# Three-term float32r products for Wo, W4 and the last layer in a one-core GNN kernel, with graph operations, one-hot turns and warm-up matmuls moved

## Chip, cores and metric

One core of a Trainium2 chip (trn2) runs the whole program. The metric is the device time of one execution in microseconds (us). Differences of 0.2% are the finest that are spoken of.

## What is computed

Four graph layers in sequence on 128 nodes with 512 features and 4096 edges, each followed by a layer norm over `x + layer(x)`. All values are float32. Cut to what the change touches:

```python
# layer 0: attention over the graph (8 heads of 64), then
attn_out = attn_out @ Wo + bo
h1 = layer_norm(x + attn_out, g1, be1)
ff = relu(h1 @ W1 + b1) @ W2 + b2
# layer 1: edge network: h = mish(edge_feat @ W1 + b1); messages = mish(h @ W2 + b2)
agg = segment_sum(messages, dst)
u = mish(concat([x, agg]) @ W3 + b3)
out = u @ W4 + b4                      # then layer_norm(x + out)
# layer 2: two GCN convolutions, 512 -> 128 -> 512, with the normalised adjacency
# layer 3:
h_self = einsum("nd,od->no", x, W_self)
h_neigh = einsum("nd,od->no", neigh_mean, W_neigh)
h = layer_norm(h_self + h_neigh + bias) * gamma + beta
```

## The kernel before

The program is written by hand, one instruction list for each engine (`block.sync`, `block.gpsimd`, `block.scalar`, `block.tensor`, `block.vector`), and semaphores join them. There is no scheduler: each engine does its list in the order in which it stands in the code, and a wait holds everything behind it on that engine. Node rows lie on the 128 partitions. A matrix of 512 by 512 lies as four chunks of 128 rows.

**Kinds of product.** `columns_by(banks, lhs, rhs, h, cs, ...)` (L460 to L465) multiplies transposed activations by the half `h` (256 columns) of a weight matrix, over the chunks `cs`; a whole product of 512 by 512 is eight such matmuls, four for each half of the output. With float32 operands each matmul is two instructions in the trace. In the edge network the operands have already been split: a value v becomes `hi`, which is v rounded to float32r, and `lo = v - hi`, also written as float32r, and a product is the three terms hi·hi, hi·lo and lo·hi (L674 and L675, 512 columns a matmul, one instruction each). ScalarE writes the hi parts, VectorE subtracts for the lo parts.

**Start.** Five bf16 matmuls on the identity run on TensorE before x has arrived (`keep_warm(5, bank[2])`, L526, waiting for `ident_ready`); then come x transposed (L444), x added to the output banks (L458), Q and K (L537), the scores, V (L561), the counting of edges (L549), and the attention output (L573, L577), whose signal is `ao_done`.

**Around Wo.** VectorE copies the attention output in two halves (`aoT`, L927). TensorE turns one group of one-hots of the targets in the meantime (`turn_onehots(Dbf, range(1))`, L582), adds the bias rows (L584) and multiplies by Wo in float32 (L589), then turns the other seven groups (L594). Each group goes into one of four banks, ScalarE copies it to `DT` (L313), and group g (from 4 on) waits for the copy of group g - 4. VectorE, behind the two copies, does `features_low(0)` (L906), `Wclo` (L930), eight small operations on the graph matrices (L932 to L939), and only then the statistics of the first layer norm (L823), for which `wo_done` is awaited. GpSimd takes the inverse roots, the graph's first and then the norms' (L278 to L280).

**Edge network.** Eight groups of 512 edges, from 69 to 205 us. TensorE runs nearly without a pause in it.

**Tail.** u @ W4 in float32 (L748), a sum of G1 (L755), then W_self and W_neigh are turned by TensorE in eight steps (`turn`, L696), each copied by ScalarE (`turned_out`, L414), with the transposes of y between; the GCN layer (L767 to L783); then five warm-up matmuls (L787), the transposes of x (L452), the neighbour mean (L790), and the last layer in float32: `xT` by `WsT` (L795) and `nmT` by `WnT` (L798), whose inputs VectorE copies (L811, L1094). The rest is VectorE's norm and the store.

Buffers lie over each other in one region of 95 units of 512 columns; the maps are `first`, `other`, `last`.

```python
            for h in range(2):
                pe.wait_ge(S["ao_ready"], h + 1)
                for b in range(2):
                    done = columns_by(O_BANKS, aoT, Wo, b, (2 * h, 2 * h + 1), None, KC - 1)
```

Of the kernel before, what the change touches and what calls it, by code (L numbers as in the profile page):

```python
# [4 lines left out]
F32 = mybir.dt.float32  # L5
# [35 lines left out]
def gnn_kernel(nc, a, out):  # L41

    ctx = ExitStack()
    with ctx:
# [32 lines left out]
        ones2 = sb("ones2", [2, N], F32R)  # L77
        uniform = sb("uniform", [P, N])
# [25 lines left out]
        last = overlay(("W3", 0, 8, F32), ("W4", 8, 4, F32), ("WsR", 12, 4, F32), ("WnR", 16, 4, F32),  # L104
                       ("WsT", 32, 4, F32), ("WnT", 36, 4, F32), ("uT", 40, 1, F32), ("aggT", 41, 1, F32), ("agg_sb", 42, 1, F32),
                       ("nmT", 43, 1, F32), ("xb_late", 44, 1, F32), ("r1g", 45, 1, F32), ("p1g", 46, 1, F32), ("r0", 47, 1, F32),
                       ("G1", 78, 1, F32), ("G2", 79, 1, F32))

        thin = overlay(("bvo", 87, 2, F32), ("bvo_parts", 89, 2, F32R))
        ctx.enter_context(nc.sbuf_tensor("region", [P, 95 * D], F32))  # L110
# [8 lines left out]
        qT, kT, aoT = (chunks(first["MA"][:, i * D:(i + 1) * D], KC) for i in (0, 1, 3))  # L119
# [17 lines left out]
        WsT, WnT, uT, aggT, nmT = (chunks(last[n], KC) for n in ("WsT", "WnT", "uT", "aggT", "nmT"))  # L137
# [43 lines left out]
        for name in ("x_in ids_in row_ids_in0 row_ids_in1 st_ready vecs_in ea_in wq_in0 wq_in1 wq_in2 wq_in3 wk_in0 wk_in1 wk_in2 wk_in3 ids_twice wv_in wo_in f1_in f2_in w1_in wc_in w2_in w3_in w4_in g_in ws_in wn_in b1g_in "  # L181
                     "out_stored consts ident_ready ident_bf_ready x_transposed xT_ready cols_done cols_ready q_done k_done v_done "
                     "qk_ready v_ready onehot_bf ct_done ct_read uniform_ready eighth ea_done ea_hi ea_lo wc_hi wc_lo bvo_in bvo_hi bvo_parts sign_ready scores_done s_centred exp_done attn_ready ao_done ao_ready wo_done "
# [5 lines left out]
                     "ones_ready sum_done sum_ready y2_ready y2T_done y2T_ready z_done r0_ready g1_done g1_ready g2_done g2_ready g3_done nm_done nm_ready l3_done wt_done wt_ready y_centred y_final0 y_final1 "  # L189
# [75 lines left out]
        def _(pool):  # L265
# [12 lines left out]
            inverse_root(1, small[:, 1:2], small[:, 2:3], S["deg_ready"], S["dinv_ready"])  # L278
            for n in range(8):
                inverse_root(n + 1, mv[:, 1:2], rstd[:, :], S["stat_ready"], S["rstd_ready"])  # L280


        @block.scalar
        def _(act):
# [109 lines left out]
            for g in range(G):  # L394
# [11 lines left out]
                message(g, 3)  # L406

            for j in range(KC):
                act.wait_ge(S["u_done"], j // 2 + 1)
                bias_out(uT[:, j, :], quarter(bank[5 if j >= 2 else 7], j), "L1_gnn_b3", j, ACT.Mish).then_inc(S["u_ready"], 1)  # L410
# [8 lines left out]
            for h in range(2):  # L419
                act.wait_ge(S["y2T_done"], h + 1)  # L420
                act.activation(half(flat(xT[:, :, :]), h), (bank[2], bank[4])[h][:, 0:D // 2], ACT.Copy).then_inc(S["y2T_ready"], 1)
            turned_out(range(TURNED_FIRST, 2 * KC))
            act.wait_ge(S["g1_done"], 1)
            act.activation(r1g, bank[3][:, 0:HID2], ACT.Relu).then_inc(S["g1_ready"], 1)
            act.wait_ge(S["g2_done"], 1)
            act.activation(p1g, bank[4][:, 0:N], ACT.Copy).then_inc(S["g2_ready"], 1)


            act.wait_ge(S["y_centred"], 1)
# [694 lines left out]
```

## Time and profile before

| | |
|---|---|
| median of 3 runs | 244.22 us (243.98 to 244.51) |
| profiled execution, its own time | 244.86 us |
| its span in the trace | 243.1 us |
| TensorE busy | 230.7 us, 95%, 1230 instructions |
| VectorE busy | 155.0 us, 64% |
| ScalarE busy | 121.5 us, 50% |
| GpSimd busy | 5.5 us, 2% |

The page gives the busy time of each engine, the chain of work that ended last, and groups of instructions. PE is TensorE's matmuls, PEld its weight loads, DVE VectorE, ACT ScalarE, POOL GpSimd, SPq the queue of SyncE. `x16` behind a float32 product of eight matmuls counts its sixteen instructions. A busy time holds the drain of the last matmul, so the pace of a stream is better read from the chain, in which each piece ends where the next begins.

### The profile page before, as it was taken

Reading aid. Unit: us, or ns where it says so; the run is one execution under the profiler, and the core shown is the slowest. Engines: PE = TensorE matmul, PEld = TensorE weight load, DVE = VectorE, ACT = ScalarE, POOL = GpSimd, SP = SyncE. Lnnn points to the kernel's source line nnn. Section 1 sums busy time; section 2 is a strip of 40 time slices with the busy share of each in tenths; the row PEclk is TensorE's granted clock in tenths of the full one; section 3 lists DMA queues with packets and bytes.
Section 4 is the critical chain, followed back from the end, with each engine's and each line's share of the span. In section 5 each row is a group of like instructions: output and inputs, shape, how many; then the busy total and the mean of one; then the engine's idle time right before and its main releaser. Section 6 shows DMA issues by size and latency. Waiting matters only on the chain.

```text
span 243.1 us, 3227 instructions
## 1 busy us (share of the span) xinstructions
PE 230.7 (95%) x1230; PEld 185.8 (76%) x1230; DVE 155.0 (64%) x274; ACT 121.5 (50%) x221; POOL 5.5 (2%) x17
## 2 busy tenths in 40 slices
PE   7999999997999999999999999999999999997980
PEld 4977888664766887888888888888888889996760
DVE  3948765687679655865856848758568455273625
ACT  0617289748639835745635646456356343244000
POOL 0000000001000000000000000000000000000001
PEclk9999999999999999999999999999999999999996
DMA  7999969920580000008041040140000000000001
GB/s 231 288 411 396 391 188 385 380 79 0 167 260 7 0 0 0 3 17 325 3 118 59 0 174 0 10 165 0 0 0 3 0 0 0 3 0 0 3 1 43
DMA packets 12039, 24.97 MB, mean 103 GB/s; under 512 B 988, under 2 KB 1908, under 8 KB 11640
## 3 DMA queue, kind: packets, MB, share of 16 engines
q1 hardware_dynamic: 11232, 24.25, 28.3%
q10 hardware_dynamic: 792, 0.51, 0.8%
q8 instruction: 10, 0.16, 0.3%
q14 instruction: 5, 0.04, 0.1%
HBM read 24.50 MB, written 0.26 MB: 102 GB/s over the span
## 4 chain that ended last, share of the span: by engine, by line
PE 89%; DVE 4%; ACT 2%; issue 2%; POOL 1%; POOLq 0%; DVEq 0%; ACTq 0%
PE bank L675 36%; PE bank L658 12%; PE bank L463 9%; PE bank L472 6%; PE bank L521 4%; PE bank L537 3%; PE bank L685 3%; PE bank L686 3%; PE bank L561 1%; PE bank L482 1%; PE bank L452 1%; ACT WsT L414 1%; PE bank L637 1%; PE bank L549 1%; PE bank L638 1%
## 5 line engine op out<-in xcount | busy, mean ns | idle before, releaser
L675 PE MATMUL bank<-W2hi,Hhi 128*128 128x512 f32 x128 | 49.8, 389 | 0.0
L675 PE MATMUL bank<-W2lo,Hhi 128*128 128x512 f32 x128 | 49.8, 389 | 0.0
L675 PE MATMUL bank<-W2hi,Clo 128*128 128x512 f32 x128 | 49.8, 389 | 0.0
L386 ACT ACTIVATE Mhi<-M 128x512 fp32r<-128x512 f32 x32 | 20.2, 632 | 45.4 <-DVE M L1011 45.4
L1016 DVE TENSOR_TENSOR Mlo<-M,Mhi 128x512 fp32r<-128x512 f32 x32 | 22.1, 689 | 24.4 <-ACT M L387 24.4
L1011 DVE TENSOR_TENSOR M<-bank,b2r 128x512 f32<-128x512 f32 x32 | 22.0, 687 | 12.7 <-PE bank L686 7.6
L675 PEld LDWEIGHTS bank<-W2hi,Hhi 128*128 128x128 f32 x128 | 24.0, 188 | 5.1
L675 PEld LDWEIGHTS bank<-W2lo,Hhi 128*128 128x128 f32 x128 | 24.0, 188 | 5.0
L675 PEld LDWEIGHTS bank<-W2hi,Clo 128*128 128x128 f32 x128 | 24.0, 188 | 5.0
L379 ACT ACTIVATE Hhi<-C 128x512 fp32r<-128x512 f32 x32 | 20.0, 624 | 12.4 <-DVE C L997 12.1
L297 ACT ACTIVATE C<-bank,cols 128x512 f32<-128x512 f32 x32 | 19.9, 685 | 10.5 <-PE bank L521 10.5
L997 DVE TENSOR_TENSOR C<-bank,C 128x512 f32<-128x512 f32 x32 | 21.4, 689 | 5.1 <-PE bank L658 4.1
L1002 DVE TENSOR_TENSOR Clo<-C,Hhi 128x512 fp32r<-128x512 f32 x32 | 22.0, 687 | 3.7 <-ACT C L380 3.7
L658 PE MATMUL bank<-ST,AB 128*128 128x512 f32 x64 | 20.0, 399 | 0.0
L380 ACT ACTIVATE C<-C 128x512 f32<-128x512 f32 x32 | 19.8, 618 | 0.0
L387 ACT ACTIVATE M<-M 128x512 f32<-128x512 f32 x32 | 19.7, 616 | 0.0
L658 PE MATMUL bank<-DT,AB 128*128 128x512 f32 x64 | 19.4, 390 | 0.0
L658 PEld LDWEIGHTS bank<-ST,AB 128*128 128x128 f32 x64 | 11.6, 188 | 3.9 <-DVE C L997 1.0
L658 PEld LDWEIGHTS bank<-DT,AB 128*128 128x128 f32 x64 | 12.0, 188 | 2.6
L685 PE MATMUL bank<-Mhi,Dg 128*128 128x512 f32 x32 | 12.6, 395 | 0.0
L686 PE MATMUL bank<-Mlo,Dg 128*128 128x512 f32 x32 | 12.5, 389 | 0.0
L276 POOL TENSOR_TENSOR rstd<-mv,mhalf 128x1 f32<-128x1 f32 x8 | 4.4, 549 | 207.4 <-DVE mv L853 194.7
(201 smaller groups left out, 315.5 us busy)
## 6 DMA issues: line engine op xcount, KB each, us to landing
F<-in_L_gnn_W SPq DMA_DIRECT2D x2, 2048.0 KB, 14.6
W1raw<-in_L_gnn_W SPq DMA_DIRECT2D x1, 2048.0 KB, 23.7
ids<-in_src SPq DMA_DIRECT2D x2, 1024.0 KB, 13.1
W<-in_L_gnn_W SPq DMA_DIRECT2D x1, 2048.0 KB, 9.1
Wq<-in_L_gnn_Wq SPq DMA_DIRECT2D x4, 256.0 KB, 3.7
Wk<-in_L_gnn_Wk SPq DMA_DIRECT2D x4, 256.0 KB, 5.4
Wv<-in_L_gnn_Wv SPq DMA_DIRECT2D x1, 1024.0 KB, 9.6
ea<-in_edge_attr SPq DMA_DIRECT2D x1, 1024.0 KB, 11.6
```

The costliest lines, as they stand in the source:

```text
L297: return act.activation(dst, src, func, bias=cols[:, col[name] + j:col[name] + j + 1])
L379: act.activation(Hhi[:, g % 2, j, :], C[:, g, j, :], ACT.Mish)
L380: act.activation(C[:, g, j, :], C[:, g, j, :], ACT.Mish).then_inc(S["h_hi"], 1)
L386: act.activation(Mhi[:, t, :], M[:, t, :], ACT.Mish)
L463: done = mm(banks[h][:, 0:D // 2], lhs[:, c, :], rhs[:, c, D // 2 * h:D // 2 * (h + 1)], start=c == start, stop=c == stop)
L658: done = mm(ST1[u % 3][:, :], w[:, P * j:P * (j + 1)], x[:, GE * g:GE * (g + 1)], start=k == 0, stop=k == len(terms) - 1)
L675: done = mm(ST2[t][:, :], x[:, c, e], w[:, c, :], start=c == 0 and i == 0, stop=c == KC - 1 and i == 2)
L685: mm(AGG[:, :], Dg[:, t, :], Mhi[:, t, :], start=g == 0 and t == 0, stop=False)
L997: v.tensor_tensor(C[:, g, j, :], ST1[u % 3][:, :], C[:, g, j, :], ALU.add).then_inc(S["z1_read"], 1)
L1002: v.tensor_tensor(Hlo[:, g, j, :], C[:, g, j, :], Hhi[:, g % 2, j, :].bitcast(F32), ALU.subtract).then_inc(S["h_lo"], 1)
L1011: v.tensor_tensor(M[:, t, :], ST2[t][:, :], row["L1_gnn_b2"], ALU.add).then_inc(S["z2_read"], 1)
L1016: v.tensor_tensor(Mlo[:, t, :], M[:, t, :], Mhi[:, t, :].bitcast(F32), ALU.subtract).then_inc(S["m_lo"], 1)
```

## The change

- **W4, the last layer and Wo** become three-term float32r products. ScalarE writes `Wohi`, `aoThi`, `W4hi`, `uThi`, `WsThi`, `WnThi`, `xThi`, `nmThi`; VectorE writes the lo parts. The W4 parts are made inside groups 5 to 7 of the edge network. A product of 8 matmuls in float32 (16 instructions) becomes 24 matmuls of 256 columns.
- **Target turns**: all eight groups stand behind Wo on TensorE.
- **Graph operations**: VectorE does them behind the first norm and `features_low(2)`; GpSimd's inverse root for them stands behind the first norm's.
- **Softmax**: the sum over heads is done by adds in place of two reductions; ScalarE copies `CTs` ahead of `uniform`; the load of the mish table stands behind `Wchi`.
- **Warm-up**: six matmuls on a tile of ones that VectorE sets first of all, in place of five on the identity.

```diff
@@ scalar
             act.wait_ge(S["ct_done"], 1)
+            act.activation(CTs[:, :], bank[0][:, 0:N], ACT.Copy).then_inc(S["ct_read"], 1)
             act.wait_ge(S["eighth"], 1)
             act.activation(uniform[:, :], bank[0][:, 0:N], ACT.Relu, bias=eighth[:, 0:1], scale=-1.0 / HEADS).then_inc(S["uniform_ready"], 1)
-            act.activation(CTs[:, :], bank[0][:, 0:N], ACT.Copy).then_inc(S["ct_read"], 1)
-            act.preload_act_table_set("mish")
+            act.wait_ge(S["wo_in"], 16)
+            for c in range(KC):
+                act.activation(Wohi[:, c, :], Wo[:, c, :], ACT.Copy).then_inc(S["wo_hi"], 1)
+            act.wait_ge(S["ao_done"], 1)
+            for h in range(2):
+                act.activation(half(flat(aoThi), h), half(bank[3], h), ACT.Copy).then_inc(S["ao_hi"], 1)
+            features_high(0)
             act.wait_ge(S["wc_in"], 32)
             act.activation(Wchi, Wc, ACT.Copy).then_inc(S["wc_hi"], 1)
-            features_high(0)
+            act.preload_act_table_set("mish")
...
+                if g in (G - 3, G - 2):
+                    act.wait_ge(S["w4_in"], 16)
+                    for c in range(2):
+                        c += 2 * (g - G + 3)
+                        act.activation(W4hi[:, c, :], W4[:, c, :], ACT.Copy).then_inc(S["w4_hi"], 1)
...
@@ tensor
+            pe.wait_ge(S["warm_ready"], 1)
+            keep_warm(6, bank[2])
             pe.wait_ge(S["ident_ready"], 1)
-            keep_warm(5, bank[2])
...
-            turn_onehots(Dbf, range(1))
             for b in range(2):
                 mm(O_BANKS[b][:, 0:D // 2], ones2[:, :], bvo_parts[:, D + D // 2 * b:D + D // 2 * (b + 1)], start=False, stop=False)
-            pe.wait_ge(S["wo_in"], 16)
-            for h in range(2):
-                pe.wait_ge(S["ao_ready"], h + 1)
-                for b in range(2):
-                    done = columns_by(O_BANKS, aoT, Wo, b, (2 * h, 2 * h + 1), None, KC - 1)
...
-            turn_onehots(Dbf, range(1, G))
+            for h in range(2):
+                pe.wait_ge(S["ao_hi"], h + 1)
+                pe.wait_ge(S["wo_hi"], 2 * (h + 1))
+                for b in range(2):
+                    columns_by(O_BANKS, aoThi, Wohi, b, (2 * h, 2 * h + 1), None, None)
+            for h in range(2):
+                pe.wait_ge(S["ao_lo"], h + 1)
+                for b in range(2):
+                    columns_by(O_BANKS, aoTlo, Wohi, b, (2 * h, 2 * h + 1), None, None)
+            pe.wait_ge(S["wo_lo"], KC)
+            for b in range(2):
+                columns_by(O_BANKS, aoThi, Wolo, b, range(KC), None, KC - 1).then_inc(S["wo_done"], 1)
...
+            turn_onehots(Dbf, range(G))
...
+            for h in range(2):
+                pe.wait_ge(S["xl_hi"], h + 1)
                 for b in range(2):
-                    columns_by((bank[4], bank[0]), xT, WsT, b, (2 * h, 2 * h + 1), None, None)
+                    columns_by(out_banks, xThi, WsThi, b, (2 * h, 2 * h + 1), None, None)
...
+            for b in range(2):
+                for c in range(KC):
+                    pe.wait_ge(S["wn_lo"], c + 1)
+                    done = columns_by(out_banks, nmThi, WnTlo, b, (c,), None, KC - 1)
+                done.then_inc(S["l3_done"], 1)
@@ vector
-                step = v.tensor_reduce(quarter(y, o), attn[:, o].rearrange("p j n -> p n j"), AX.X, ALU.add)
+                pairs, four = half(y, 1), quarter(y, o)
+                chain(v.tensor_tensor(pairs, attn[:, o, 0:2].rearrange("p j n -> p (j n)"), attn[:, o, 2:4].rearrange("p j n -> p (j n)"),
+                                      ALU.add))
+                chain(v.tensor_tensor(four, quarter(pairs, 0), quarter(pairs, 1), ALU.add))
...
+            wo_low((0, 1))
+            for h in range(2):
+                dve.wait_ge(S["ao_hi"], 2)
+                v.tensor_tensor(half(flat(aoTlo), h), half(bank[3], h), half(flat(aoThi), h).bitcast(F32), ALU.subtract).then_inc(S["ao_lo"], 1)
+            wo_low((2, 3))
```

TensorE around Wo, before: L577 ends the attention output, L496 turns one-hots, L584 adds the bias rows, L463 is Wo.

```order
13 L577 MATMUL bank<-attn,MA 64x128 x8
14 L496 MATMUL bank<-ident_bf,Dbf 128x128 x4
15 L584 MATMUL bank<-bvo_parts,ones 128x256 x2
16 L463 MATMUL bank<-Wo,MA 128x256 x8
17 L496 MATMUL bank<-ident_bf,Dbf 128x128 x28
18 L503 MATMUL bank<-ident,ea 128x128 x4
19 L452 MATMUL bank<-ident,y 128x128 x4
```

The same place in the changed kernel:

```order
13 L619 MATMUL bank<-attn,MA 64x128 x8
14 L623 MATMUL bank<-bvo_parts,ones 128x256 x2
15 L505 MATMUL bank<-Wohi,aoThi 128x256 x8
16 L505 MATMUL bank<-Wohi,aoTlo 128x256 x8
17 L505 MATMUL bank<-Wolo,aoThi 128x256 x8
18 L537 MATMUL bank<-ident_bf,Dbf 128x128 x32
19 L544 MATMUL bank<-ident,ea 128x128 x4
20 L494 MATMUL bank<-ident,y 128x128 x4
```

All 32 turns now stand between Wo and the transposes of y, where 28 stood.

ScalarE in the tail of the changed kernel, from the copies of the turned weights on (before, no row with a `hi` tile stood here):

```order
177 L444 ACTIVATE WsT<-bank 128x512 x4
178 L444 ACTIVATE WnT<-bank 128x512
179 L451 ACTIVATE xT<-bank 128x256 x2
180 L439 ACTIVATE WsThi<-WsT 128x512 x2
181 L444 ACTIVATE WnT<-bank 128x512 x3
182 L456 ACTIVATE r1g<-bank 128x128
183 L439 ACTIVATE WsThi<-WsT 128x512
184 L459 ACTIVATE p1g<-bank 128x128
185 L439 ACTIVATE WsThi<-WsT 128x512
186 L463 ACTIVATE WnThi<-WnT 128x512 x4
187 L466 ACTIVATE xThi<-bank 128x256 x2
188 L468 ACTIVATE nmThi<-bank 128x512
```

Two rounding copies stand ahead of the last three turned weights, and one between `r1g` and `p1g`, which the GCN layer needs in turn.

VectorE from the GCN layer's norm to the last statistics, changed kernel:

```order
221 L900 BN_STATS stats<-bank 128x6 x2
222 L1195 BN_AGGR mv<-stats 128x2
223 L1117 TENSOR_TENSOR WsTlo<-WsT,WsThi 128x512
224 L1199 TENSOR_SCALAR xs<-bank,mv,rstd 128x256 x2
225 L1204 TENSOR_TENSOR xTlo<-bank,xThi 128x256 x2
226 L1207 TENSOR_TENSOR nmTlo<-bank,nmThi 128x512
227 L1117 TENSOR_TENSOR WsTlo<-WsT,WsThi 128x512
228 L1117 TENSOR_TENSOR WnTlo<-WnT,WnThi 128x512 x4
229 L1211 TENSOR_TENSOR xs<-xs,rows 128x512
230 L900 BN_STATS stats<-bank 128x6 x2
```

Before, the two copies of `xT`, one of `nmT` and the sum `xs` were all that stood between the norm and the statistics; now five subtractions on weights stand there too.

## Rows read from the trace of the kernel before

**Rows 1.** The page: TensorE's share, and the chain that ended last by engine.

```profile
PE 230.7 (95%) x1230; PEld 185.8 (76%) x1230; DVE 155.0 (64%) x274; ACT 121.5 (50%) x221; POOL 5.5 (2%) x17
...
PE 89%; DVE 4%; ACT 2%; issue 2%; POOL 1%; POOLq 0%; DVEq 0%; ACTq 0%
```

**Rows 2.** Chain that ended last, tail: start us, length us, piece.

```profile
167.37 8.16 PE bank L675 x36
...
207.73 3.84 PE bank L472 x32
211.57 3.46 PE bank L463 x16
215.03 0.89 PE bank L755 x8
...
216.39 2.07 ACT WsT L414 x4
...
229.01 6.92 PE bank L463 x32
236.03 0.44 DVE stats L823
```

**Rows 3.** The same chain around Wo.

```profile
25.90 3.65 PE bank L463 x16
...
31.44 0.40 PE bank L496 x4
...
33.35 3.84 PE bank L472 x32
```

**Rows 4.** The same chain at the start.

```profile
1.66 2.31 PE bank L482 x5
3.97 0.85 PE bank L444 x4
4.82 1.71 PE bank L458 x4
6.53 4.00 PE bank L537 x32
10.70 3.77 PE bank L537 x32
...
15.75 3.63 PE bank L561 x8
```

**Rows 5.** Timeline of TensorE, the only float32r matmuls of 256 columns (bias rows).

```profile
25.40 0.29 PEld L584 LDWEIGHTS bank<-bvo_parts,ones 2*128 2x128 f32 x2
25.40 0.50 PE L584 MATMUL bank<-bvo_parts,ones 2*128 2x256 f32 x2
```

**Rows 6.** Timeline of ScalarE and VectorE, edge network: [idle before <- releaser].

```profile
194.50 0.63 ACT L386 ACTIVATE Mhi<-M 128x512 fp32r<-128x512 f32 x1 [2.83 <-DVE M L1011]
...
189.19 0.69 DVE L1016 TENSOR_TENSOR Mlo<-M,Mhi 128x512 fp32r<-128x512 f32 x1 [1.22 <-ACT M L387]
```

**Rows 7.** Timeline of ScalarE in the GCN layer: r1g and p1g.

```profile
222.55 0.28 ACT L424 ACTIVATE r1g<-bank 128x128 f32<-128x128 f32 x1 [0.22 <-PE bank L774]
...
223.47 0.28 ACT L426 ACTIVATE p1g<-bank 128x128 f32<-128x128 f32 x1 [0.64 <-PE bank L777]
```

**Rows 8.** Timeline of VectorE and ScalarE around Wo.

```profile
25.18 0.76 DVE L927 COPY MA<-bank 128x256 f32<-128x256 f32 x2 [1.18 <-PE bank L577]
25.85 0.68 DVE L906 TENSOR_TENSOR EATlo<-bank,EAThi 128x512 fp32r<-128x512 f32 x1
...
29.65 0.43 DVE L823 BATCH_NORM_STATS2 stats<-bank 128x6 f32<-128x256 f32 x1 [0.50 <-PE bank L463]
...
29.81 3.54 ACT L313 ACTIVATE DT<-bank 128x512 fp32r<-128x512 f32 x7 [3.70 <-PE bank L496]
```

**Rows 9.** The tile Wv: its load, and the time from issue to landing.

```profile
L223 SPq DMA_DIRECT2D Wv<-in_L_gnn_Wv x1: 482/482/482, 5.0 to 5.0; - x1
...
DMA to landing us min/median/max: 9.6/9.6/9.6
```

More of the change, by code:

```diff
@@ L77, in gnn_kernel @@
         ones2 = sb("ones2", [2, N], F32R)
+        warm = sb("warm", [P, P], BF16)
         uniform = sb("uniform", [P, N])
@@ L118, in gnn_kernel @@
         F1, F2, ffT, W1raw = chunks(first["F1"], KC), chunks(first["F2"], FC), chunks(first["ffT"], FC), chunks(first["W1raw"], 2 * KC)
-        qT, kT, aoT = (chunks(first["MA"][:, i * D:(i + 1) * D], KC) for i in (0, 1, 3))
+        qT, kT = (chunks(first["MA"][:, i * D:(i + 1) * D], KC) for i in (0, 1))
+        Wohi, Wolo, aoThi, aoTlo = (chunks(wo_split[n], KC) for n in ("Wohi", "Wolo", "aoThi", "aoTlo"))
         v_sb = first["MA"][:, 2 * D:3 * D]
@@ L136, in gnn_kernel @@
         W3, W4, WsR, WnR = chunks(last["W3"], 2 * KC), chunks(last["W4"], KC), chunks(last["WsR"], KC), chunks(last["WnR"], KC)
-        WsT, WnT, uT, aggT, nmT = (chunks(last[n], KC) for n in ("WsT", "WnT", "uT", "aggT", "nmT"))
+        WsT, WnT, uT, aggT = (chunks(last[n], KC) for n in ("WsT", "WnT", "uT", "aggT"))
+        W4hi, WsThi, WnThi, xThi, xTlo, nmThi, nmTlo, uThi = (chunks((late if n == "WsThi" else last)[n], KC) for n in (
+            "W4hi", "WsThi", "WnThi", "xThi", "xTlo", "nmThi", "nmTlo", "uThi"))
+        W4lo, WsTlo, WnTlo, uTlo = (chunks(rest[n], KC) for n in ("W4lo", "WsTlo", "WnTlo", "uTlo"))
         G1, G2 = chunks(last["G1"], KC), last["G2"]
@@ L1066, in _ @@
             v.memset(ones, 1.0).then_inc(S["ones_ready"], 1)
+            for h in range(2):
+                dve.wait_ge(S["u_hi"], 2 * (h + 1))
+                dve.wait_ge(S["u_ready"], 2 * (h + 1))
+                v.tensor_tensor(half(flat(uTlo), h), half(flat(uT), h), half(flat(uThi), h).bitcast(F32), ALU.subtract).then_inc(S["u_lo"], 1)
             st = residual((bank[2], bank[4]), xw, S["o_done"])
@@ L1071, in _ @@
             v.bn_aggr(mv[:, :], statistics(y[:, :])).then_inc(S["stat_ready"], 1)
+            weight_low(WsTlo, WsT, WsThi, (0,), "ws")
             dve.wait_ge(S["stat_ready"], norms[0])
@@ L1088, in _ @@
                                        op0=ALU.mult, op1=ALU.add).then_inc(S["xw_ready"], 1)
-            norm((bank[5], bank[6]), xs[:, :], S["nx_ready"], bank_statistics((bank[5], bank[6]), S["g3_done"]))
-            out_halves(xT_flat, (bank[1], bank[3]), S["nT_done"], 4, S["nT_ready"])
-            dve.wait_ge(S["nm_done"], 1)
-            v.tensor_copy(flat(nmT), bank[2][:, :]).then_inc(S["nm_ready"], 1)
+            weight_low(WsTlo, WsT, WsThi, (1,), "ws")
+            st = bank_statistics((bank[5], bank[6]), S["g3_done"])
+            norms[0] += 1
+            v.bn_aggr(mv[:, :], st).then_inc(S["stat_ready"], 1)
+            weight_low(WsTlo, WsT, WsThi, (2,), "ws")
+            dve.wait_ge(S["stat_ready"], norms[0])
+            dve.wait_ge(S["rstd_ready"], norms[0])
+            halves(lambda d, x, h: v.tensor_scalar(d, x, mv[:, 0:1], rstd[:, 0:1], ALU.subtract, ALU.mult), xs[:, :],
+                   (bank[5], bank[6]), S["nx_ready"])
+            for h in range(2):
+                dve.wait_ge(S["xl_hi"], h + 1)
+                v.tensor_tensor(half(flat(xTlo), h), (bank[1], bank[3])[h][:, 0:D // 2], half(flat(xThi), h).bitcast(F32),
+                                ALU.subtract).then_inc(S["xl_lo"], 1)
+            dve.wait_ge(S["nm_hi"], 1)
+            v.tensor_tensor(flat(nmTlo), bank[2][:, :], flat(nmThi).bitcast(F32), ALU.subtract).then_inc(S["nm_lo"], 1)
+            weight_low(WsTlo, WsT, WsThi, (3,), "ws")
+            weight_low(WnTlo, WnT, WnThi, range(KC), "wn")
             dve.wait_ge(S["nx_ready"], 6)
```

120 lines of the change are left out of this document (85 added, 35 removed).

## The prediction

> **What bounds the kernel now.** I read the page's shares first, then the chain that ended last in order of time, then timelines at the places that the change touches. TensorE is busy for 95% of the span and makes 89% of the chain [rows 1], so a saving counts where TensorE's own stream gets shorter at a place on the chain, and where nothing else becomes the last to arrive. Three touched places lie on the chain: W4 and the last layer [rows 2], Wo [rows 3], and the start [rows 4]. The reader should see that W4's 16 instructions take 3.46 us, 0.216 each, that the last layer's 32 take 6.92 us at the same pace, and that VectorE's statistics follow at once at 236.03.
>
> **Pace of the new matmuls.** This is the size on which most hangs. No row shows a stream of float32r matmuls of 256 columns with full weights. Nearest from above: 36 float32r matmuls of 512 columns in 8.16 us, 0.227 each, of which 0.213 would be columns at the pace of 0.416 ns each that float32 gets (512 column steps in 0.216 less a few ns), so some 0.013 is a cost per instruction [rows 2]. Half the columns: 0.107 + 0.013 = 0.12. From the other side: the two bias matmuls, float32r with 256 columns, have weight loads that together take 0.29 where one alone takes 0.18, so the second starts 0.11 later, and both matmuls end at 25.90, a pace near 0.12 [rows 5]. A stream of 32 float32 instructions with 128 columns each, which also stream for 0.107, takes 3.84 us, 0.12 each, with a new full weight load for every one [rows 2]. So I take 0.12, with bounds of 0.11 (loads as close as rows 5) and 0.135 (between these rows and the 0.144 at which 24 matmuls cost the same 3.46). By the Trainium skill's page "TensorE: Matmul & The Clock Gate", section "Back-to-back issue gap", N columns cost N/2.4 + 2.5 ns, that is 109 ns here; the two products of the tail would then gain 2.5 us together, not the 1.7 that follows.
>
> **W4.** 16 x 0.216 = 3.46 becomes 24 x 0.12 = 2.88: TensorE is done 0.58 sooner. The operands must be there: W4's four rounding copies (0.63 each) and subtractions (0.69 each) go into groups 5 to 7 of the edge network, where ScalarE idles 2.83 us at the border of a group and VectorE 1.22 us for each message [rows 6]; two copies or one subtraction fit, cost nothing. The lo part of u's first half is not needed until eight hi matmuls (0.96) have run; ScalarE and VectorE make it in 0.6 + 0.4. For the second half the order hi·hi, hi·lo, lo·hi gives the same cover. After W4 the chain does not go through VectorE but through L755 and ScalarE's copies of turned weights [rows 2], which start as soon as TensorE is free, so the 0.58 passes on. VectorE's branch gains only 0.2 (its first half ends after 20 of 24 matmuls, 2.40, against 12 of 16, 2.59), but it had about 0.7 to spare. What is late next: ScalarE has `WsThi` copies between. Two stand behind the copies of xT and ahead of three weight copies, which TensorE awaits only at L777. One stands between r1g and p1g: they lie 0.92 apart, r1g takes 0.28 [rows 7], so 0.64 is free for a copy of 0.63. It fits with nothing left; a delay of 0.1 is what I allow.
>
> **Last layer.** 32 x 0.216 = 6.92 becomes 48 x 0.12 = 5.76: 1.16 sooner. The first use of `nmThi` is after 16 matmuls (1.9 us), and needs one copy of 0.63. VectorE must then do `nmTlo`, `WsTlo` chunk 3 and four `WnTlo`, six subtractions with a start every 0.60 (in rows 8, 25.85 follows two copies of 0.38 begun at 25.18, and 0.68 is the whole length). Counted from the start of the product at 0, nmTlo starts at 0.9, the last subtraction ends at about 4.6, the sum xs at 5.2, and the first half of the output is done at 44 x 0.12 + 0.17 = 5.45. So VectorE is ready 0.2 before TensorE, and TensorE, which takes WnTlo last, chunk by chunk from 4.8 on, finds it there. At a pace of 0.11 VectorE is the bound and only 0.2 more is gained. From the statistics on nothing is changed.
>
> **Wo.** TensorE's stream would be 0.58 shorter, but its inputs now come later and what follows is bound by others. `ao_done` is at 25.18 [rows 8]. ScalarE rounds two halves (0.38 each, as VectorE's copies there), until 25.9; VectorE then subtracts two halves (until 26.6) and two chunks of Wo (until 27.9; the first two are made before, while TensorE is in the attention output). The last eight matmuls start at 27.9 and end at 29.0, against 29.55 [rows 3]. But ScalarE then copies eight groups of one-hots where seven were left: it starts 0.26 behind the end of Wo, at 29.3, against 29.81, with a copy every 0.49 (3.54 for seven, the last 0.6) [rows 8]. The last group of turns waits for the fourth copy, now 29.3 + 3 x 0.49 + 0.6 = 31.4; before, that group ran at 31.44 [rows 3]. VectorE has `features_low(0)` and `Wclo` (0.6 each) ahead of the statistics, so the second one starts at 29.5, against 29.65 [rows 8]. Hence the transposes of y and the F1 product at 33.35 [rows 3] stay where they are: **zero**, with ends of -0.3 and +0.4. The graph operations, eight small ones on VectorE, go to where it waits for W1hi, and cost nothing; the softmax adds shorten a stretch after which VectorE waits for the edge counts anyway, and `uniform`, which now comes after `CTs`, takes back that lead. I put both at 0.
>
> **Start.** The first five matmuls take 0.43 each, which is the 1.2 GHz level, L444 and L458 run at half pace too, and the 32 instructions of Q take 4.00 where those of K take 3.77, so the clock rose about 7.3 [rows 4]. TensorE now begins at about 0.95 in place of 1.66, and six warm-ups are over at 3.5, before x is there at about 3.7, so the transposes start 0.1 sooner. If the clock rises where it did, that 0.1 is all. If it rises 0.7 sooner, as the first matmul does, 0.7 us of half-speed work shrinks by 0.35. If it rises before x, over 1.5 us could go, but V waits for Wv, which lands at 5.0 + 9.6 = 14.6 [rows 9] and starts at 15.75 [rows 4]: at most 1.05. I take the middle: 0.1 + 0.35, rounded to 0.4, ends 0.1 and 1.05. Loads behind it (Wo, F1, W1) land with over 1 us to spare.
>
> **Sum.** 0.58 + 1.16 + 0 + 0.4 = 2.15 us. The profiled execution took 244.86 (span 243.1 and 1.8 around it), so it would take 242.7; the median of the runs is 0.64 below the profiled one, which gives 242.1.
>
> **Rivals.**
> 1. *The clock does not rise sooner.* For: x arrives when it did, and the rise lay far behind the first matmul. Against: nothing in the rows ties it to a place. Gain 0.58 + 1.16 + 0.1: 242.4. Chance 0.25.
> 2. *The clock rises before Q*, and V waits for Wv: gain 1.74 + 1.05: 241.4. Chance 0.15.
> 3. *The splits become the bound.* p1g late by a copy (0.3 to 0.6) and VectorE's row of subtractions at their full 0.69, or Wo's ring later: some 1 us of the gain is lost: 243.1. For: margins of 0.0 and 0.2. Chance 0.15.
> 4. *Weight loads are not hidden under short float32r matmuls*, the case in which the kernel gets slower. A full load (0.107 of streaming) and then a matmul (0.12) in series make 0.227. Then W4 takes 5.45 for 3.46, the last layer 10.9 for 6.92, Wo some 1.5 more: about +7, 251. It decides from a pace of 0.144 on. Against it: the float32 stream of 128 columns at 0.12 a piece, each with a new full load [rows 2]; if loads were in series it would take 0.21. For: no float32r stream shows it with full rows. Chance 0.04. The Trainium skill's same page, section "The mechanism" of Part 3, says that a weight load overlaps with matmuls in flight only when the row groups differ; by that rule this rival would come true, and the L472 row speaks against it.
> 5. *The three-term products do not shorten the chain at all*, since VectorE's norms set the ends. Against: VectorE waits for TensorE at L823 [rows 8], and the chain is TensorE's. 244.0. Chance 0.03.
>
> **Numbers.** The forecast itself (0.38) lies between 241.7 and 242.5; with rivals 1 to 3 the range from 241.0 to 243.3 holds over eight in ten. About 0.2% (0.5 us) is what a measurement of this kernel can tell from no change. Faster by more: 0.91, from the forecast and rivals 1, 2 and most of 3; within: 0.04; slower: 0.05.
>
> **What would show it.** The chain should have the W4 stretch at 2.9 us for 24 instructions and the last layer at 5.8 for 48; a pace over 0.135 refutes the main term. The F1 product should start as far behind the attention output as before (33.35 - 25.18 = 8.2). p1g should follow L777 at once, and the last statistics follow TensorE, not a subtraction. The start of V tells the clock's part: 15.3 by my forecast, 14.7 by rival 2, 15.65 by rival 1. The forecast falls if the last layer waits for WnTlo or if DT copies end later than the norm's transposes can bear.

## The result, and the profile after

The changed kernel takes 243.17 us (median of 20 runs), the kernel before 244.28 (20 runs beside it). The ratio is 0.9962, 95% interval 0.9949 to 0.9975: 0.9 us faster by the ratio, 1.1 by the medians, where 2.15 were forecast. A later set gave 0.9952 (0.9935 to 0.9969). The profiled execution took 243.27, its span is 241.4.

The page of the changed kernel, shares by engine, against [rows 1]:

```profile
PE 228.5 (95%) x1263; PEld 184.1 (76%) x1263; DVE 165.0 (68%) x295; ACT 132.7 (55%) x246; POOL 5.9 (2%) x17
...
PE 82%; DVE 4%; DMA 4%; ACT 3%; issue 2%; SPq 2%; POOL 1%; POOLq 0%; DVEq 0%; ACTq 0%
```

TensorE has lost 2.2 us of work, VectorE and ScalarE have gained 10 and 11. New on the chain is a DMA, the load of Wv. The chain of the changed kernel (start us, length us, piece), against [rows 2 to 4]:

```profile
5.09 9.84 DMA Wv<-in_L_gnn_Wv
14.97 3.70 PE bank L603 x8
25.84 1.21 DVE Wolo L1007 x2
27.09 1.22 PE bank L505 x8
28.59 2.07 ACT DT L325 x4
32.61 3.84 PE bank L514 x32
...
207.00 3.84 PE bank L514 x32
210.84 2.88 PE bank L505 x24
215.09 2.07 ACT WsT L444 x4
...
228.14 5.29 PE bank L505 x44
...
234.00 0.44 DVE stats L900
```

The two large terms are there: W4 takes 2.88 for 24 instructions where it took 3.46 for 16, and the last layer runs at 5.29 / 44 = 0.120 each where it ran at 0.216. Now go from place to place and subtract. V starts 0.78 sooner by the pieces of the two chains (0.70 by its first matmul), F1 0.74, W4 0.73, the turned weights on ScalarE 1.30. (V is the attention's value product, F1 the first feed-forward product.) So far it fits, if the start is worth its 0.7. The last product, though, starts 0.87 sooner, not 1.3. The chain between, in the changed kernel:

```profile
224.47 0.25 DVE mv L1195
224.72 0.07 issue
224.79 0.88 POOL rstd L287
225.66 0.03 issue
```

and in the kernel before:

```profile
225.73 0.25 DVE mv L846
225.98 0.07 issue
226.05 0.56 POOL rstd L276
226.60 0.03 issue
```

GpSimd's inverse root for the third norm, the same instruction on the same 128 values, takes 0.32 longer. The timeline of VectorE and GpSimd in the changed kernel shows its neighbour:

```profile
224.47 0.24 DVE L1195 BATCH_NORM_AGGREGATE mv<-stats 128x2 f32<-128x18 f32 x1
224.63 0.63 DVE L1117 TENSOR_TENSOR WsTlo<-WsT,WsThi 128x512 fp32r<-128x512 f32 x1
224.79 0.87 POOL L287 TENSOR_TENSOR rstd<-mv,mhalf 128x1 f32<-128x1 f32 x1 [6.10 <-DVE mv L1195]
```

The subtraction of WsT's chunk 2 is placed there by the change; the forecast priced it at nothing, as work in VectorE's idle time. The root ends 0.40 behind it.

**Three sections of the program.** Executions of one kernel differ by some tenths of a us and more, most of it ahead of V. So I cut each profile at two marks: the first matmul of V, and the start of the second (last half's) statistics of the last norm, which is `236.03` in [rows 2] and 234.00 here. From V to the mark: 236.03 - 15.68 = 220.35 before, 234.00 - 14.97 = 219.03 after, that is -1.32. From the mark to the end of the span: 7.0 before, 7.4 after. The last section is the same code and takes 0.3 longer. I took this for scatter at first; the table at the end of the experiments shows that it is not.

### The profile page after: what moved, and what is told of

Read it like the earlier page. It is cut to its first block, busy times and chain, and to the rows that moved or that the text cites. A ratio compares the mean times of both kernels' runs of the same rounds, so it can differ in the third digit from the quotient of the medians.

```text
span 241.4 us, 3347 instructions
## 1 busy us (share of the span) xinstructions
PE 228.5 (95%) x1263; PEld 184.1 (76%) x1263; DVE 165.0 (68%) x295; ACT 132.7 (55%) x246; POOL 5.9 (2%) x17
## 4 chain that ended last, share of the span: by engine, by line
PE 82%; DVE 4%; DMA 4%; ACT 3%; issue 2%; SPq 2%; POOL 1%; POOLq 0%; DVEq 0%; ACTq 0%
PE bank L721 36%; PE bank L704 12%; PE bank L505 7%; PE bank L514 6%; PE bank L562 4%; DMA Wv<-in_L_gnn_Wv 4%; PE bank L731 3%; PE bank L732 3%; PE bank L603 2%; PE bank L494 1%; ACT DT L325 1%; ACT WsT L444 1%; PE bank L683 1%; POOL rstd L287 1%; PE bank L591 1%
```

## Experiments

Two accounts were put against each other. The first: the product terms are whole; the start brings almost nothing in most executions, because the one profile of before that I read was one with a late clock; 0.33 is lost at the root. The second: the product terms arrive only in part. The profiled time of each run, its sections and its ratio stand in one table below; here is what each decided.

### The kernel before, once more

No edit.

> The kernel before once more, unchanged, for a second profile of its start and for the noise. Theory A (its first profile fell on an execution with a late clock): the span is some 0.5 us under 243.1, V starts nearer to Wv's landing than the 1.0 us of the first profile, and the ratio is 1.000. Theory B: V again starts 1 us behind the landing.

Ratio 1.0002 (0.9989 to 1.0014). Its chain at the start, against [rows 4]:

```profile
1.66 2.32 PE bank L482 x5
4.83 1.23 PE bank L458 x4
6.06 3.57 PE bank L537 x32
9.80 3.77 PE bank L537 x32
13.58 1.27 PE bank L556 x16
14.85 3.63 PE bank L561 x8
```

Q's 32 instructions take 3.57 and L458's four 1.23, where the first profile had 4.00 and 1.71. The traces record when the granted clock goes from the lower to the upper of its two levels (1.2 and 2.4 GHz): at 7.31 in the first profile and at 5.45 in this one, before L458's matmuls were over. The kernel is the same. Its V starts 0.9 sooner, more than the whole change of the start was to bring. From V to the mark it takes 220.33 against 220.35: that section repeats to a few hundredths.

### The start alone, undone and done

Undone in the changed kernel:

```diff
-            pe.wait_ge(S["warm_ready"], 1)
-            keep_warm(6, bank[2])
             pe.wait_ge(S["ident_ready"], 1)
+            keep_warm(5, bank[2])
```

> The changed kernel with the start of before: five warm-up matmuls on the identity, no tile of ones. Theory A (the start gives the median run little, because V waits for Wv in most executions with either start, and only executions in which TensorE's clock rises late gain): median at most 0.2 us above the changed kernel's 243.2, and a profile in which V starts either right at Wv's landing or up to 1 us behind it. Theory B (the start gives its 0.4 to 0.8 us in every execution, and what is missing was lost elsewhere): 243.6 to 244.0.

Ratio 0.9966 (0.9953 to 0.9979), beside 0.9962 with the new start. The median is 243.60, which lies in theory B's range, 0.4 above the changed kernel's; but the kernel before, run beside each, differs too, and the two ratios differ by only 0.1 us. This run alone decides neither way. Done in the kernel before (the same lines the other way round):

> The kernel before with one piece of the change: six warm-up matmuls on a bfloat16 tile of ones that VectorE sets, ahead of the identity, in place of five on the identity. Everything else as before. Theory A (in most executions V's first matmul waits for Wv or for x, not for the clock): 244.2 to 244.4, ratio 0.999 to 1.001. The prediction's term (-0.4, with the clock rising some 2.5 us sooner and V at 15.3 or earlier in every execution): 243.9, ratio 0.9984 or lower. Its other end (-1.05): 243.3.

244.05, ratio 0.9996 (0.9983 to 1.0009). The forecast's 0.9984 is just inside the interval, its end of -1.05 is excluded. What the medians leave open, all runs together narrow down. The span of each run is on record, and from V to the end a kernel takes the same time to 0.05 (table below), so the span less that section is an estimate of when V began. Over 100 runs with the old start the mean is 15.11, over 127 with the new one 14.97: the new start is worth 0.14, give or take 0.1. It is an estimate, since each kernel's section is taken from its one profile; the forecast's 0.4 lies outside it.

In the profile of the changed kernel V waits for Wv, issued at 5.09 and landed 9.84 later, so a clock that rises sooner still meets that bound. V starts 0.04 behind Wv's landing in nine of the seventeen profiles with the new start and in one of the three with the old one. The clock's rise lies at 5.40, 5.45 and 7.31 with the old start, and anywhere from 4.17 to 6.98 with the new one.

### The root of the third norm

Chunk 2's subtraction moved ahead of the statistics:

```diff
-            weight_low(WsTlo, WsT, WsThi, (1,), "ws")
+            weight_low(WsTlo, WsT, WsThi, (1, 2), "ws")
             st = bank_statistics((bank[5], bank[6]), S["g3_done"])
             norms[0] += 1
             v.bn_aggr(mv[:, :], st).then_inc(S["stat_ready"], 1)
-            weight_low(WsTlo, WsT, WsThi, (2,), "ws")
```

> The changed kernel with the subtraction for WsTlo chunk 2 moved from beside GpSimd's inverse root of the third norm to the place of chunk 1, ahead of the statistics. Theory A (VectorE's subtraction of two SBUF tiles holds GpSimd's root up for 0.32 us, on the chain): the root takes 0.55 us again in place of 0.87, and the median falls by 0.3, to 242.85. Theory B (the root is long for another reason, or the norm's scaling is held by VectorE itself): the root stays at 0.87 or the median does not move by more than 0.1.

The root takes 0.55 again, V to the mark 218.70 instead of 219.03, ratio 0.9947 (0.993 to 0.9964). The median did not move: 243.16, where theory A said 242.85. The two stretches decide it, since they repeat to 0.02: the subtraction beside the root costs 0.33. Which operations do this? Six variants of what stands beside the root:

> The changed kernel with one subtraction, that of chunk 2 of WsT's low part beside GpSimd's third inverse root, written as a scalar_tensor_tensor (times 1.0, minus) instead of a tensor_tensor: same tiles, same place, same two inputs in SBUF. Theory A1 (it is the form of the operation that holds GpSimd up: in this kernel's own trace a scalar_tensor_tensor with two SBUF inputs lies beside an inverse root at 57.22 and again at 215.4, and the root lasts 0.55 both times): the root goes from 0.87 to 0.55, V to the last statistics from 219.03 to 218.7, ratio about 0.995. Theory A2 (any VectorE operation with two SBUF inputs does it, and the two old cases escaped by their timing): root 0.87, ratio 0.996 as the changed kernel.

> The changed kernel with one wait moved: VectorE waits for its own bn_aggr of the third norm before, not behind, the subtraction of WsT's chunk 2, so that the subtraction starts some 0.1 later, about 0.05 ahead of GpSimd's inverse root instead of 0.16 ahead of it. Theory A3 (the root is held up only by a VectorE operation that is already under way; in the trace of the changed kernel the two operations that start 0.05 ahead of a root, at 56.50 and 215.39, do not lengthen it): root 0.55 instead of 0.87, the subtraction about 0.65, V's first matmul to the last statistics 219.03 - 0.3 = about 218.7. Theory A2 (any two-input VectorE operation of this kind beside the root holds it up to its own end): root 0.9 to 1.0, since the subtraction ends 0.1 later, and V to the statistics 219.1.

> The changed kernel with the subtraction beside the third inverse root as a scalar_tensor_tensor whose scalar is a column of ones in SBUF instead of the immediate 1.0 or a plain tensor_tensor. Theory A4 (the norms' own operations escape because their scalar comes from a tile, which takes another path through VectorE and leaves GpSimd its port): root 0.55 and the operation some 0.77 long, as the norms' are. Theory A5 (the scalar plays no part; the output's type or something else does): root 0.85 or longer, ending about 0.4 behind the subtraction's end.

> The changed kernel with chunk 2 of WsT's low part ahead of the third norm's statistics, and in its old place beside the inverse root one tensor_tensor of the same size and inputs (chunk 3) whose float32 output goes to a tile that nobody reads any more. Theory A6 (the float32r output is what makes it hold GpSimd up): root 0.55. Theory A5b (a tensor_tensor with two SBUF inputs does it whatever its output's type): root 0.85 or longer, V to the statistics 219.0 as in the changed kernel.

> The changed kernel with chunk 2 of WsT's low part ahead of the third norm's statistics, and beside the third inverse root, behind VectorE's wait for its bn_aggr, one extra scalar_tensor_tensor of the norms' own form (tile minus mv, times the row of L1's gamma, in place) on a tile that nobody reads any more. If the form decides: root 0.55, as at 56.50 and 215.39 in the changed kernel's trace, and the operation 0.77 long. If the place decides (something about this third root): root about 1.05, its end 0.4 behind the operation's end, as with the subtraction that started as late.

> As the run before it in this set, but the second input is chunk 2 of WsT's high part instead of the row of L1's gamma. If the second input's tile decides: root about 1.0 here and 0.55 there. If the pair of operations or the scalar of mv decides: 0.55 in both.

The subtraction that starts 0.1 later (e10), timeline of VectorE and GpSimd:

```profile
224.28 0.69 DVE L1117 TENSOR_TENSOR WsTlo<-WsT,WsThi 128x512 fp32r<-128x512 f32 x1
224.33 1.05 POOL L287 TENSOR_TENSOR rstd<-mv,mhalf 128x1 f32<-128x1 f32 x1 [6.11 <-DVE mv L1195]
```

With a column of ones as its scalar (e14), and with a float32 output (e16):

```profile
224.42 0.68 DVE L1197 SCALAR_TENSOR_TENSOR WsTlo<-WsT,r,WsThi 128x512 fp32r<-128x512 f32 x1
224.59 0.93 POOL L287 TENSOR_TENSOR rstd<-mv,mhalf 128x1 f32<-128x1 f32 x1 [6.11 <-DVE mv L1195]
```

```profile
224.13 0.63 DVE L1197 TENSOR_TENSOR agg_sb<-WsT,WsThi 128x512 f32<-128x512 f32 x1
224.29 0.86 POOL L287 TENSOR_TENSOR rstd<-mv,mhalf 128x1 f32<-128x1 f32 x1 [6.12 <-DVE mv L1195]
```

In the norms' own form, with WsThi as second input (e18):

```profile
224.81 0.77 DVE L1197 SCALAR_TENSOR_TENSOR agg_sb<-agg_sb,mv,WsThi 128x512 f32<-128x512 f32 x1
224.85 0.55 POOL L287 TENSOR_TENSOR rstd<-mv,mhalf 128x1 f32<-128x1 f32 x1 [6.11 <-DVE mv L1195]
```

In every held case the root ends 0.40 to 0.41 behind VectorE's operation, whenever that ends (225.26 and 225.65 in the changed kernel, 224.97 and 225.38 in e10, 224.90 and 225.30 in e7): as if most of its 0.55 could not run until that operation was done. Several guesses fell. An operation that starts only 0.05 ahead of the root holds it too (e10), so does one whose scalar is a tile (e14), and one with a float32 output (e16); with WsThi as its second input the norms' own form still holds nothing (e18). What e17 and e18 have and the held ones have not was not taken apart further: minus and then times, in place, with mv, the tile that the root reads, as the scalar. Their operation takes 0.77, the held ones 0.63 to 0.69. It starts 0.04 ahead of the root, as in e10, so the order of the two does not tell them apart. Both are single runs; the changed kernel's trace has the same form beside two other roots, at 56.50 and 215.39, and these take 0.55 as well. Why the form escapes stays open.

The Trainium skill's page "SBUF — State Buffer", section "Who interferes with whom", says that a VectorE instruction with two SBUF inputs contends with a GpSimd instruction that reads SBUF, that the lock on the shared ports is exclusive, and that the order of issue decides who is blocked. The changed kernel, e7, e10, e14 and e16 agree, with 0.31 to 0.50 as the price; e17 and e18 have two SBUF inputs too and cost nothing, and there the measurement differs from the page.

### Wo

Back to float32, with the first turn group ahead of it and the table load ahead of Wc, as before:

```diff
+            turn_onehots(Dbf, range(1))
...
-                pe.wait_ge(S["wo_hi"], 2 * (h + 1))
...
-                    columns_by(O_BANKS, aoThi, Wohi, b, (2 * h, 2 * h + 1), None, None)
...
+                    done = columns_by(O_BANKS, aoT, Wo, b, (2 * h, 2 * h + 1), None, KC - 1)
...
-            turn_onehots(Dbf, range(G))
+            turn_onehots(Dbf, range(1, G))
```

> The changed kernel with Wo as before: float32, the copy of the attention output on VectorE, the table load and the first group of turns ahead of Wo. Theory A (the three-term Wo gains nothing, since the copies of the turned one-hots and VectorE set the start of the next product): 8.2 us from the end of the attention output to F1, the median within 0.15 of 243.2. Theory B (the three-term Wo gains its 0.58 us): 243.7.

From the end of the attention output to F1: 8.20, against 8.26 in the changed kernel and 8.21 before. Wo in three terms, as the change orders it, brings nothing, as forecast at 0. The ratio is 0.9938 (0.9921 to 0.9956) and the median 242.62, below what either theory said; V to the mark is only 0.10 shorter. The table below has the rest, in the exit. Then the other half of that piece, the moved turns:

```diff
             done.then_inc(S["ao_done"], 1)
+            pe.wait_ge(S["ident_bf_ready"], 1)
+            pe.wait_ge(S["cols_ready"], 1)
+            turn_onehots(Dbf, range(1))
...
-            turn_onehots(Dbf, range(G))
+            turn_onehots(Dbf, range(1, G))
```

with ScalarE's copy of group 0 between `features_high(0)` and `Wchi`, and chunk 2 ahead of the statistics as in e2. In e9 `Wclo` is moved behind LN1 as well; e15 leaves it.

> The changed kernel with chunk 2 of WsT's low part ahead of the third norm's statistics, Wclo's subtraction behind LN1's work, and the first group of one-hot turns back ahead of the three-term Wo product, its copy by ScalarE between the splits. Theory A (Wo's three terms gain nothing because TensorE waits for the splits and the four turn groups behind them, so a group in that gap helps): attention output's end to the first F1 matmul 8.26 - 0.3 = about 8.0, V to the statistics 218.4. Theory B (LN1's chain of VectorE and the DT copies by ScalarE set the stage whatever TensorE does first): 8.2 to 8.3 and 218.7. Theory C (the copy ahead of Wc's split delays ScalarE's queue): 8.4 or more.

> The changed kernel with chunk 2 of WsT's low part ahead of the third norm's statistics and the first group of one-hot turns ahead of the three-term Wo product; Wclo's subtraction stays where the change has it. Theory A (the four turn groups behind Wo, and ScalarE's four copies behind them, are what ate the gain of the three-term Wo): attention output's end to the first F1 matmul 7.8, V to the statistics 218.2, ratio 0.9925. Theory B (it was Wclo's subtraction ahead of LN1's statistics that did it, moved as well in the run that had 7.77): 8.2, and 218.6, ratio 0.994.

The ratio of e9 is 0.9925 (0.9907 to 0.9944). From the attention output to F1: 7.77 in e9, 7.80 in e15, against 8.26: it is the turn group, not `Wclo`. Timeline of ScalarE in e15:

```profile
25.39 0.62 ACT L325 ACTIVATE DT<-bank 128x512 fp32r<-128x512 f32 x1
...
28.55 3.54 ACT L325 ACTIVATE DT<-bank 128x512 fp32r<-128x512 f32 x7 [0.73 <-PE bank L538]
```

and in the changed kernel:

```profile
28.59 4.03 ACT L325 ACTIVATE DT<-bank 128x512 fp32r<-128x512 f32 x8 [1.23 <-PE bank L537]
```

ScalarE has eight copies behind Wo in the changed kernel, one every 0.49, and TensorE's turns wait for its banks; with one copy done in the gap before, the seven left end 0.5 sooner, and F1 starts 0.46 sooner. So three-term Wo is worth 0.4 on this stretch (8.20 to 7.80), and the moved turn group gives it all back.

### W4 and the last layer, undone one by one and together

W4: `columns_by(..., uT, W4, ...)` in place of the three terms, without the split of W4 and u.

> The changed kernel with the W4 product back in float32: 8 matmuls instead of 24, no split of W4 and u; the last layer, Wo and the start stay as changed. Theory A (the terms W4 -0.58 and last layer -1.16 are whole, and +0.33 is lost at the third norm's inverse root on GpSimd): the stretch of the W4 product goes from 2.88 back to 3.46, the time from V's first matmul to the last layer's statistics from 219.03 to about 219.6, and the median from 243.17 to about 243.75 (ratio to the kernel before 0.9975). Theory B (only half of what the rows show arrives in the time, so the two terms were over-counted): 243.4 to 243.5, because W4's split has taken back some of it elsewhere, and the stretch from V to the statistics grows by 0.3 or less.

The last layer: the same with `xT, WsT` and the neighbour mean with `WnT`.

> The changed kernel with the last layer back in float32 (16 matmuls instead of 48, no split of WsT, WnT, x and the neighbour mean); W4, Wo and the start stay as changed. Theory A: the last product lasts 6.9 instead of 5.3 to 5.8, but the subtraction of WsT's low part beside GpSimd's inverse root is gone too, so the root is back at 0.55 and 0.33 comes back: V to the last statistics 219.03 + 1.16 - 0.33 = about 219.85, median about 244.0. Theory B (the longer root has nothing to do with the subtraction, for instance it follows from the earlier order of GpSimd's own work): the root stays at 0.87, V to the statistics 220.2, median about 244.3.

Both:

> The changed kernel with W4 and the last layer both back in float32: what is left of the change is the start, Wo in three terms, the graph operations behind LN1 and the moved turns. The forecast's terms for these: start -0.4, Wo 0, so 243.8 and a ratio of 0.998. Theory A (start about 0 in most executions, the Wo stage +0.04, the extra copy ahead of the uniform term included): ratio 0.9993 to 1.0003, V's first matmul to the last statistics 220.3 less about 0.1, root 0.55, since the subtraction beside it is gone too.

Stage by stage the terms are whole: from the turned aggregate's product to the next product behind W4, 7.13 with W4 in float32 and 6.55 with three terms (0.58). From the last product's start on, undoing the last layer costs 1.08 and the root gives 0.32 back, V to the mark +0.78 for a forecast of +0.83. But the times do not follow: undoing W4 left the median at 243.18, where theory A said 243.75, and undoing the last layer at 243.61, where it said 244.0. With both undone the median is 244.38 and the ratio 1.0008 (0.9995 to 1.002), above theory A's range, and V to the mark is 220.68 where about 220.2 was expected.

### The sum is in the last section

Each kernel's profile cut at the two marks; "end" is from the mark to the end of the span; V to end is the sum, and "less before" is that sum less the kernel before's. The ratio column is the measured difference, and its interval is about 0.4 to either side.

| kernel | V to mark | root | end | V to end | less before | ratio x 244.3 - 244.3 | median |
|---|---|---|---|---|---|---|---|
| before, twice | 220.35, 220.33 | 0.55 | 7.0, 7.0 | 227.4, 227.4 | | | 244.3 |
| e8 before, new start | 220.33 | 0.55 | 7.0 | 227.3 | 0.0 | -0.1 | 244.05 |
| changed, twice | 219.03, 219.01 | 0.87 | 7.4, 7.4 | 226.4, 226.4 | -1.0 | -0.9, -1.2 | 243.17, 242.89 |
| e1 old start | 218.96 | 0.87 | 7.4 | 226.4 | -1.0 | -0.8 | 243.60 |
| e2 root | 218.70 | 0.55 | 7.4 | 226.1 | -1.3 | -1.3 | 243.16 |
| e3 Wo float32 | 218.92 | 0.86 | 7.0 | 226.0 | -1.4 | -1.5 | 242.62 |
| e5 W4 float32 | 219.47 | 0.87 | 7.0 | 226.5 | -0.9 | -1.0 | 243.18 |
| e6 last layer float32 | 219.81 | 0.55 | 7.0 | 226.8 | -0.6 | -0.5 | 243.61 |
| e13 both float32 | 220.68 | 0.55 | 7.0 | 227.7 | +0.3 | +0.2 | 244.38 |
| e7, e14, e16 beside root | 218.99, 219.02, 218.96 | 0.86 to 0.93 | 7.4 | 226.4 | -1.0 | -1.2, -1.0, -1.2 | 242.93, 243.34, 243.08 |
| e10 subtraction later | 219.06 | 1.05 | 7.4 | 226.5 | -0.9 | -1.2 | 243.35 |
| e17, e18 norms' form | 218.68, 218.67 | 0.55 | 7.4 | 226.1, 226.0 | -1.3 | one run each | 242.67, 242.90 |
| e9 turn, root, Wclo | 218.19 | 0.55 | 7.4 | 225.6 | -1.8 | -1.8 | 242.77 |
| e11 root, Wo float32 | 218.51 | 0.55 | 7.0 | 225.5 | -1.8 | -1.8 | 242.53 |
| e15 turn, root | 218.18 | 0.55 | 7.4 | 225.6 | -1.8 | -2.1 | 242.33 |

The columns "less before" and the measured one agree within 0.3 in every line. The "end" has two values and nothing between: 7.0 in the eight profiles of kernels whose trace has 297 to 315 ScalarE records (before, and each in which Wo, W4 or the last layer is undone), 7.4 in the twelve profiles with all three splits, 321 records. The code behind the mark is the same. In the trace's record of ScalarE's queue the last instruction but one, a DRAIN, starts 0.43 to 0.46 behind the branch that ends the wait for the output, and takes 0.09 to 0.10; in the other eight it starts 0.16 to 0.18 behind and takes 0.01. SyncE's DRAIN stands 0.15 behind its branch in all. So the third split makes the exit 0.33 to 0.36 longer, whichever of the three it is. The count of records does not say which engine it hangs on (VectorE has 357 to 359 in the twelve and 333 to 354 in the eight, TensorE's counts part in the same way); the late DRAIN points to ScalarE. The loading of instructions is a suspect: in all twelve a DMA packet of the kind "instruction" starts 0.6 to 0.9 behind that DRAIN, in the eight none does within 1.9. But that is a coincidence in time and no test, and no run took it apart; the cause is open.

Once more the changed kernel, and the combination of e2 and e3:

> The changed kernel once more, unedited, so that the others of this set have it beside them on the same chip. Theory A: ratio 0.996 within its interval, V's first matmul to the last statistics 219.03 within 0.05, whatever the time at which V starts (14.9 to 16.1 in the profiles so far). Theory B (the stretch differs from execution to execution as much as between the kernels, so the stage sums above prove nothing): another value by 0.2 or more.

> The changed kernel with two parts taken back that the runs so far show to cost or to bring nothing: chunk 2 of WsT's low part is subtracted ahead of the third norm's statistics, and the Wo product is float32 again with the first group of one-hot turns ahead of it. W4, the last layer, the order of the graph operations and the start stay as changed. Theory A: root 0.55, V to the last statistics 219.03 - 0.33 - 0.10 = 218.6, ratio to the kernel before 0.9935 to 0.995, median 242.7 to 243.0, ahead of the changed kernel. Theory B (what the trace shows on this stretch does not arrive in the time): 243.1 to 243.2, as the changed kernel.

219.01 and 0.9952: theory A, V to the mark holds whatever V's start (14.97 and 14.74 here). e11 comes to 0.9927 (0.9911 to 0.9943), e15 to 0.9916 (0.9899 to 0.9933) with the lowest median, 242.33, 0.6 to 1.1 us ahead of the changed kernel by medians and ratios. Their intervals overlap, and from V to the end they are equal, 225.5 and 225.6: three-term Wo with its turn group ahead gains 0.33 up to the mark over float32 Wo, and the longer exit takes it back. So no run shows that Wo's three terms pay in this kernel at all. e15 with the exit of e11 was not tried.

e13 has a surprise of its own. The chain behind its third root:

```profile
225.09 0.56 POOL rstd L287
225.65 0.03 issue
225.68 0.02 DVEq L1142
225.70 0.40 issue
226.10 0.56 DVE xs L1143
```

VectorE stands still for 0.40 of "issue", where the same step has 0.05 in the changed kernel. That is about the 0.33 by which this kernel is behind before from V to the mark. Without it Wo and order would come to 0. What it waits for the trace does not say; here too an "instruction" packet follows, 0.9 behind the end of the pause.

## Why the prediction was wrong

**Right:** the pace of short float32r matmuls. 0.12 was taken, 5.29 / 44 = 0.120 was measured; W4 brought 0.58 and the last layer 1.1 to 1.16 (by e6, and by the stages of the profile), as costed. The 109 ns a matmul that the prediction sets beside its own 0.12, and the gain of 2.5 us that would follow from it, did not come: 0.120 and 1.74. Rival 4 (weight loads in series, 0.227 a piece) is out: it gave 16 us for the two stretches together, they took 8.6. The rule of the Trainium skill's page "TensorE: Matmul & The Clock Gate", section "The mechanism" of Part 3, does not hold for these streams. `WsThi` between r1g and p1g fitted into its 0.64 (221.29 and 222.21, 0.92 apart as before), and VectorE's row of subtractions ended before TensorE needed it: the last statistics waited 0.42 for TensorE. The clock's rise, read off the matmuls as about 7.3, is on record at 7.31. Wo at zero, F1 8.26 behind the attention output against 8.21.

**Wrong, first step: "Start", 0.4, over-sized.** It was worked out from one profiled execution, whose clock rose late, and the clock's rise was taken for a property of the kernel. Another profile of the same kernel had V 0.9 sooner. The two runs on the start alone put the change at 0.1 in each, with an interval of 0.3 to either side, which does not exclude 0.4; the spans of all runs put it at 0.14, give or take 0.1. That is the forecast's own lower end, the 0.1 by which the transposes start sooner. The profile after seemed to bear the step out, with V at 14.97 where 15.3 was forecast; only the second profile of before showed what such a comparison is worth. Rival 1's size was nearest. Its reading, that the rise is not tied to the first matmul, fits the rises at 4.17 to 6.98 with one and the same new start.

**Wrong, second step: the subtractions of the last layer.** "Last layer" counts those that VectorE does from the start of the product on; chunks 0 to 2 of WsT's low part, which stand ahead of it, got no price, as work in idle time. For TensorE this held. But VectorE's idle 0.66 behind the third norm's statistics is the time of GpSimd's root, and the chunk placed there holds the root up: +0.33 on the chain (e2). The prediction asked which engine is late, not what an operation beside another engine's does to that one. The row to doubt it was in view: the root is a piece of the chain, and any work beside it was new.

**Wrong, third step: "from the statistics on nothing is changed".** The code isn't, the time is: +0.33 in the program's exit once ScalarE carries all three splits (e3, e5, e6, e11, e13 against twelve profiles). Nothing in the rows of before could have told it, and its cause is open.

Sum: -0.58 - 1.16 + 0.33 + 0.33 = -1.08, with -0.14 for the start and +0.05 at Wo -1.2, against -0.9 and -1.2 measured. Rival 3 gave a time close to it (243.1), by luck and another mechanism: no split was late, one was in the way.

**Wo** was right in its number and missed what was there to be had: the forecast noted that eight copies stand behind Wo where seven did, and took it as given. e15 shows that this part was worth 0.46. That three-term Wo takes nearly as much back in the exit had no place in the forecast.

## What to carry to other kernels

Price each moved operation twice: for the engine that runs it, and for what runs beside it on an engine with which it may share a path; a filler beside a short GpSimd step on the chain is not free. When a matrix product gets shorter, ask what the neighbouring queue now has to do in one piece, and give it a part of that beforehand. And cut traces at marks that repeat (here to 0.02 us over executions that differ by 0.9 at the start): a term of 0.3 that the medians of a few runs did not show (e2) stands out, and so does one at the end that looks like scatter.

## What the runs showed that I had not expected

A subtraction of two SBUF tiles of 128x512 (0.63 to 0.69) holds GpSimd's root until 0.40 after its end (root 0.86 to 1.05 for 0.55), but the scalar_tensor_tensor "minus mv, times a tile" (0.77) does not. The exit has two lengths, 7.0 and 7.4 us behind the same mark, with the number of ScalarE's records (315 or fewer, 321). VectorE lost 0.40 at one place of one kernel (e13) with nothing in the profile that it waits for. V's first matmul starts anywhere from 14.5 to 15.5 in seventeen profiles with the new start, and the clock rises anywhere from 4.2 to 7.0.
